# A two-layer macaron transformer on eight cores: rounding written out on VectorE, bf16 quantized weights in HBM, and other orders for LayerNorm and the output projections

## The chip, the cores and the metric

One Trainium2 chip (trn2), all 8 NeuronCores. Each core computes one sequence of the batch of eight, with the same program and no exchange between cores. The metric is the device time in microseconds (us) of the slowest core.

## What is computed

```python
x = x + 0.5 * ffn0(layernorm(x))     # call 1 of ffn_l0
x = x + attn0(layernorm(x))          # 16-head softmax attention, T = 2048, D = 1024
x = x + 0.5 * ffn0(layernorm(x))     # call 2 of ffn_l0, the same weights
x = x + 0.5 * moe1(layernorm(x))     # two of eight experts are ever used
x = x + attn1(layernorm(x))          # linear attention, D_KV = 512
x = x + 0.5 * moe1(layernorm(x))

def act_quant(x):                    # per token
    scale = 127.0 / clip(max(abs(x), axis=-1), 1e-05)
    return clip(round(x * scale), -128, 127) / scale
def weight_quant(w):                 # one scale for the whole matrix, result -1, 0 or 1 times it
    scale = 1.0 / clip(mean(abs(w)), 1e-05)
    return clip(round(w * scale), -1, 1) / scale
def ffn0(x):                         # w1: 4096 x 1024, w2: 1024 x 4096
    h = act_quant(x) @ weight_quant(w1).T
    h = silu(depthwise_conv1d(h, conv_w, conv_b))      # 3 taps along the sequence
    return act_quant(h) @ weight_quant(w2).T
```

## The kernel before

The activations x_sb stay in SBUF for the whole program as 8 chunks (dc) of 128 features by 2048 tokens in f32. Everything is feature-major: a matmul has a 128x128 weight tile as its stationary operand and 512 tokens as the moving one.

Order of the work. The program is written out by hand. `em.emit` (line 47) puts each instruction on the queue of its engine with the semaphore counts it waits for. On VectorE, ScalarE and GpSimd each instruction also waits for the one before it on its own engine (`self_sems`), so on an engine nothing overlaps with its predecessor. `guard()` is a wait for everything emitted so far, the DMAs too. The weight traffic (`w1sl`, `w2sl`, `wq1s`, `wq2s`, `slg`) is issued from GpSimd's queue (POOL), in order: a DMA that waits holds back those behind it. All small helpers have one line each: tt 214, tsc 219, stt 228, cp 236, red 241, act 252, mm 208, dma 197.

LayerNorm, `emit_ln` (line 460), six times. For each of 4 groups of 512 tokens and each of 8 chunks ScalarE makes a bf16 copy and a bf16 square in the one buffer `lnscr`, and two matmuls with a column of ones (`ln_ps`) sum them; the next pair of activations waits for these two matmuls. That is 32 steps per LayerNorm. Then come the statistics per token, two broadcasts through HBM (`bcast_tok`), and two VectorE operations of 2048 columns per chunk. The tags in `res_q` let a step start when its 512 tokens are final; for this the output projections and residual adds of attn_l0, moe_l1 and attn_l1 run with the token group `qb` outside and `dc` inside.

The feed-forward block, `ffn_l0` (line 550), twice.
- Quantizing the input: the maximum per token, its broadcast, then per chunk (128x2048) two VectorE operations, a multiply with int8 output (`xi8`) and a multiply back to bf16 (`xsc1`).
- For each of 4 token groups q: the H stage, 32 steps hc. A step is 8 matmuls into `H_ps[b]` (and 8 of one column for the right neighbour of the convolution), a small copy (`hlsv`), ScalarE's scaled copy `atmp`, four VectorE operations (`t1tmp`), and ScalarE's silu into `ysilu`. Then the maximum and broadcasts, and the O stage, again 32 steps hc: VectorE multiplies to int8 (`xi2`) and back to bf16 (`xsc2[b]`), PE does 8 matmuls into the 8 banks `O_ps`. Eight residual adds end the group.
- Weight tiles come from HBM as int8, are turned to bf16 by the DMA, and are loaded for two hc at a time (`slg`, 512 KB each, two buffers; `load1`, `load2`).

The ternary weights, `prep_weight` (line 308), are made during call 1 of ffn_l0 only. Pass 1 (`s_p1`, 64 pieces of 128x512 for each of w1 and w2) sums absolute values on ScalarE; `prep_pre` emits all 128 in the middle of the input quantization. `s_fin` makes the threshold from the sum, through several small DMAs. Pass 2 (`s_p2`, again 64 + 64 pieces) compares on VectorE and stores int8 to HBM from two buffers `g8`. `prep_drain(n)` emits the next n of the steps `s_fin`, `s_p2`, `s_end`: 10 ahead of the first H stage and 4 in each step of it, so all 132 are done in the H stage of group 0:

```python
tsc("vector", H["g8"][b], H["slab"][b], H["thp"][:, 0:1], None, ALU.is_ge)
tsc("vector", H["slab"][b], H["slab"][b], H["thp"][:, 1:2], None, ALU.is_le)
tt("vector", H["g8"][b], H["g8"][b], H["slab"][b], ALU.subtract)
gcons[b] = dma(cq[b], wdst, H["g8"][b])
```

The two attention blocks and the expert block are touched only in the order of their last projection.

## Time and profile before

| | us |
|---|---|
| median of the 2 runs shown (7142.35 to 7152.05) | 7147.2 |
| the profiled execution | 7073.03 |
| its span on its slowest core, core 1 | 7071.3 |
| spans of the eight cores | 7046.3 to 7071.3 |
| VectorE busy in that span | 2659.4 |
| PE busy in that span | 3289.9 |

The profiled execution is 74.2 us shorter than the median. The span runs from the first to the last instruction. Of the profile, "idle before" is time in which an engine did nothing just ahead of such an instruction, with what ended that time. The stages of call 1 of ffn_l0 can be told by the tiles: `xi8q` input quantization, `w1g` and `w2g` pass 2, `Hps` the H stage, `xi` with `Ops` the O stage.

### The profile page before, as it was taken

To read this page: it belongs to the slowest core of one execution; us is meant where nothing else is said; L and a number is where in the kernel's file an instruction comes from. 1 tells how busy PE (TensorE), PEld (TensorE's weight loads), DVE (VectorE), ACT (ScalarE), POOL (GpSimd) and SP (SyncE) were. 2 spreads that over 40 slices of the span, in tenths; PEclk is the share of its full clock that TensorE was granted. 3 is DMA by queue.
4 is the path that set the end of the run, shared out by engine and by line. 5 is a ranking of instruction groups with operands and counts; after the bars stand their busy time and mean duration, and the time that the engine had idled before them with its cause. 6 is when DMAs were issued, how large, how long until landed. Compare 5 with 4: busy or idle time off the path is not lost.

```text
span 7071.3 us, 55121 instructions; the slowest of 8 cores (7046.3 to 7071.3 us)
## 1 busy us (share of the span) xinstructions
PE 3289.9 (47%) x13238; PEld 1250.4 (18%) x13238; DVE 2659.4 (38%) x4180; ACT 1815.5 (26%) x2752; POOL 492.8 (7%) x828
## 2 busy tenths in 40 slices
PE   2022265465255555555555432556545264344345
PEld 0000022222021112211211111222211021122012
DVE  0655655555212222122212226555653331333223
ACT  2400111211225554665466221121122002000100
POOL 0332210000000000000000000001000000000000
PEclk9965587787577667666766756778776586676568
DMA  2632322122010000000000101212211010100022
GB/s 80 183 109 83 94 84 72 44 82 67 17 12 5 7 8 10 5 5 10 8 7 2 18 12 42 66 51 81 69 48 51 29 21 11 29 8 6 12 36 60
DMA packets 142962, 290.67 MB, mean 41 GB/s; under 512 B 35106, under 2 KB 42306, under 8 KB 138050
## 3 DMA queue, kind: packets, MB, share of 16 engines
q0 software_dynamic: 129088, 240.38, 13.3%
q1 hardware_dynamic: 13572, 46.77, 2.0%
q8 instruction: 127, 2.08, 0.1%
q14 instruction: 175, 1.43, 0.1%
HBM read 229.01 MB, written 17.25 MB: 35 GB/s over the span
## 4 chain that ended last, share of the span: by engine, by line
PE 25%; DVE 23%; ACT 22%; DMA 18%; issue 10%; ACTq 1%; DVEq 1%; POOLq 0%; SPq 0%; POOL 0%
ACT aE L252 14%; DVE t1tmp L228 6%; PE Ops L208 4%; ACT lnscr L252 3%; PE meps L208 3%; DVE aden L246 3%; DMA slg<-wq2s 3%; PE Hps L208 3%; PE ln_ps L208 3%; DMA w2sl<-w2h 2%; ACT atmp L252 2%; PE aqkps L208 2%; ACT ysilu L252 2%; PE mops L208 2%; DVE sv2bc L241 2%
## 5 line engine op out<-in xcount | busy, mean ns | idle before, releaser
L208 PE MATMUL Hps<-xsc,slg 128*128 128x512 bf16 (+1 forms) x3584 | 699.6, 348 | 1037.5 <-ACT ysilu L252 439.9
L252 ACT ACTIVATE aE<-aA 128x1024 bf16<-128x1024 f32 x512 | 523.9, 1023 | 394.3 <-PE aA L208 293.3
L252 ACT ACTIVATE aE<-asps 128x1024 bf16<-128x1024 f32 x512 | 523.8, 1023 | 392.9 <-PE asps L208 334.7
L252 ACT ACTIVATE lnscr<-x_sb 128x512 bf16<-128x512 f32 x384 | 241.5, 629 | 1420.5 <-PE ln_ps L208 597.1
L252 ACT ACTIVATE atmp<-Hps,cbsb,cw2sb 128x512 f32<-128x512 f32 x256 | 198.9, 777 | 1422.5 <-DVE hlsv L236 1388.7
L208 PE MATMUL Ops<-xsc,slg 128*128 128x512 bf16 x2048 | 484.7, 391 | 151.5 <-DVE xsc L214 105.7
L208 PEld LDWEIGHTS Hps<-xsc,slg 128*128 128x128 bf16 x3584 | 292.7, 110 | 1446.0 <-issue 1314.8
L208 PE MATMUL aA<-aKp,aQp 64*128 64x512 bf16 x1024 | 387.4, 575 | 285.6 <-ACT aE L252 256.4
L208 PE MATMUL asps<-aQ,aK 65*128 65x512 bf16 x1024 | 336.2, 415 | 254.1 <-DMA aQ<-aQp 230.9
L208 PE MATMUL ln_ps<-lnscr,onesbf 128*1 128x512 bf16 x384 | 193.6, 607 | 423.0 <-ACT lnscr L252 367.7
L228 DVE SCALAR_TENSOR_TENSOR t1tmp<-Hps,cw2sb,atmp 128x511 f32<-128x511 f32 (+1 forms) x512 | 247.7, 484 | 348.6 <-ACT atmp L252 321.3
L208 PE MATMUL apps<-aE,avtok 128*65 128x512 bf16 x1024 | 328.3, 403 | 86.8 <-ACT aE L252 45.2
L252 ACT ACTIVATE ysilu<-t1tmp 128x512 f32<-128x512 f32 x256 | 161.1, 629 | 625.0 <-DVE t1tmp L228 622.3
L214 DVE TENSOR_TENSOR ad<-ad,aacc 128x1 f32<-128x1 f32 x512 | 81.7, 160 | 618.1 <-ACT aE L252 618.1
L208 PE MATMUL meps<-mxln,mew 128*128 128x512 bf16 x1024 | 230.3, 388 | 153.2 <-DMA mew<-e0T 79.9
L236 DVE CAST aden<-apps 1x512 bf16<-1x512 f32 x64 | 44.1, 689 | 649.9 <-PE apps L208 626.9
L208 PEld LDWEIGHTS Ops<-xsc,slg 128*128 128x128 bf16 x2048 | 194.2, 100 | 440.6 <-issue 250.9
L214 DVE TENSOR_TENSOR xi<-ysilu,s2bc 128x512 int8<-128x512 f32 x256 | 177.2, 692 | 223.8 <-PE Ops L208 145.3
L208 PE MATMUL aqkps<-axln,aqk 128*128 128x512 bf16 x512 | 128.8, 419 | 172.1 <-DVE aout L214 157.7
L246 DVE RECIPROCAL aden<-aden 1x2048 bf16<-1x2048 bf16 x16 | 207.1, 12944 | 1.7
L228 DVE SCALAR_TENSOR_TENSOR t1tmp<-Hps,cw2sb,t1tmp 128x511 f32<-128x511 f32 x256 | 191.8, 749 | 27.6 <-DVE t1tmp L228 1.4
L208 PEld LDWEIGHTS aA<-aKp,aQp 64*128 64x128 bf16 x1024 | 101.0, 100 | 570.6 <-issue 555.8
(181 smaller groups left out, 3754.7 us busy)
## 6 DMA issues: line engine op xcount, KB each, us to landing
slg<-wq1s POOLq DMA_DIRECT2D x128, 512.0 KB, 3.7
slg<-wq2s POOLq DMA_DIRECT2D x128, 512.0 KB, 3.7
w1sl<-w1h POOLq DMA_DIRECT2D x128, 256.0 KB, 3.1
w2sl<-w2h POOLq DMA_DIRECT2D x128, 256.0 KB, 3.1
x_sb<-x SPq DMA_DIRECT2D x8, 1024.0 KB, 5.0
out<-x_sb SPq DMA_DIRECT2D x8, 1024.0 KB, 3.9
ln_rbc<-rowbuf SPq DMA_DIRECT2D x6, 1024.0 KB
ln_mrbc<-rowbuf SPq DMA_DIRECT2D x6, 1024.0 KB
```

The costliest lines, as they stand in the source:

```text
L208: tp=tile_position: e.matmul(o, l, r, start=a, stop=b, tile_position=tp),
L214: e.tensor_tensor(o, a, b, p), wait=wait, inc=inc)
L228: p=op0, q=op1: e.scalar_tensor_tensor(o, i, s, j, p, q),
L236: em.emit(eng, lambda e, o=out_ap, i=in_ap: e.tensor_copy(o, i), wait=wait, inc=inc)
L241: e.tensor_reduce(o, i, axis=AX.X, op=p, apply_absolute_value=a),
L246: em.emit(eng, lambda e, o=out_ap, i=in_ap: e.reciprocal(o, i), wait=wait, inc=inc)
L252: s=scale, a=accum: e.activation(o, i, f, bias=b, scale=s, accum_out=a),
```

## The change

Seven edits:
- Rounding. Each int8 multiply is replaced by a chain: multiply to f32, cast to int8 (`c8`, `c82`), subtract, compare the remainder with half-integers, and add the correction. The chain has 8 operations where KL is 1 (call 1, which has `pre`) and 12 where KL is 3 (call 2); before it was 2. It is in the input quantization (128x2048) and in every step of the O stage (128x512).
- Pass 1 is a VectorE reduce instead of a ScalarE activation.
- Pass 2 has five VectorE operations instead of three, into one f32 buffer `ptmp` shared by w1 and w2, which the next piece may write only when the store of the last one has landed (`ptmp_rd`). The store turns f32 to bf16.
- The quantized weights lie in HBM as bf16, and are loaded for one hc at a time (256 KB).
- The preparation steps are emitted as 3 per step of the H stage and 2 per step of the O stage.
- LayerNorm: per chunk, VectorE copies 2048 columns and ScalarE squares 2048 columns, then 8 matmuls; 8 steps instead of 32.
- The output projections run with `dc` outside and `qb` inside; `yconv` and `amax2p` have tiles of their own.

```diff
-    wq1s = nc.dram_tensor("wq1s", [HC, 128, DC * 128], I8)
+    wq1s = nc.dram_tensor("wq1s", [HC, 128, DC * 128], BF16)
...
-                act(H["slab"][k % 2][:, :], H["slab"][k % 2][:, :],
-                    AF.Abs, accum=H["part"][:, k:k + 1],
-                    wait=[ltags[k]], inc=Ssc)
+                red("vector", H["part"][:, k:k + 1], H["slab"][k % 2][:, :],
+                    ALU.add, absval=True, wait=[ltags[k]], inc=Sdv)
...
-                tsc("vector", H["g8"][b][:, :], H["slab"][b][:, :],
-                    H["thp"][:, 0:1], None, ALU.is_ge, wait=w0, inc=Sdv)
-                tsc("vector", H["slab"][b][:, :], H["slab"][b][:, :],
-                    H["thp"][:, 1:2], None, ALU.is_le, inc=Sdv)
-                tt("vector", H["g8"][b][:, :], H["g8"][b][:, :],
+                thv = bass.AP(H["thp"], 0, [[2, 128], [0, SW]])
+                if ptmp_rd[0] is not None:
+                    w0.append(ptmp_rd[0])
+                stt("vector", ptmp[:, 0:SW], H["slab"][b][:, :], 1.0,
+                    thv, ALU.mult, ALU.subtract, wait=w0, inc=Sdv)
+                stt("vector", H["slab"][b][:, :], H["slab"][b][:, :], 1.0,
+                    thv, ALU.mult, ALU.add, inc=Sdv)
+                tsc("vector", ptmp[:, 0:SW], ptmp[:, 0:SW], 0.0, None,
+                    ALU.is_ge, inc=Sdv)
+                tsc("vector", H["slab"][b][:, :], H["slab"][b][:, :], 0.0,
+                    None, ALU.is_le, inc=Sdv)
+                tt("vector", ptmp[:, 0:SW], ptmp[:, 0:SW],
                    H["slab"][b][:, :], ALU.subtract, inc=Sdv)
...
-                gcons[b] = dma(cq[b], wdst, H["g8"][b][:, :],
+                gcons[b] = dma(cq[b], wdst, ptmp[:, 0:SW],
                                wait=[(Sdv, Sdv.c)])
+                ptmp_rd[0] = gcons[b]
...
+                    for dc in range(DC):
+                        cp("vector", scr[:, 0:T], x_sb[:, dc * T:(dc + 1) * T],
+                           wait=(g0 if dc == 0 else [(Spe, Spe.c)]), inc=Sdv)
+                        act(scr[:, T:2 * T], x_sb[:, dc * T:(dc + 1) * T],
+                            AF.Square,
+                            wait=(g0 if dc == 0 else [(Spe, Spe.c)]),
+                            inc=Ssc)
...
+                    KL = 1 if pre is not None else 3
                     for dc in range(DC):
...
+                        tt("vector", xi8[:, :], e1, s_bc[:, :], ALU.mult,
                            wait=[b2] if dc == 0 else (), inc=Sdv)
...
-                            if hc % 2 == 1 and g + 2 < 16:
-                                load1(g + 2)
+                            if hc + 2 < HC:
+                                load1(hc + 2)
...
                         for hc in range(HC):
-                            g, b = hc // 2, hc % 2
+                            if drain:
+                                drain(2)
+                            g, b = hc, hc % 2
...
+                            e1 = ysilu[:, hc * QT:(hc + 1) * QT]
+                            tt("vector", xi2[:, :], e1, s2_bc[:, :],
                                ALU.mult,
                                wait=[b2, (Spe, o_pe[b])], inc=Sdv)
+                            cp("vector", c82[:, :], xi2[:, :], inc=Sdv)
+                            tt("vector", xi2[:, :], xi2[:, :], c82[:, :],
+                               ALU.subtract, inc=Sdv)
+                            tsc("vector", e1, xi2[:, :], 0.5, None,
+                                ALU.is_gt, inc=Sdv)
+                            for j in range(1, KL):
+                                stt("vector", e1, xi2[:, :], j + 0.5, e1,
+                                    ALU.is_gt, ALU.add, inc=Sdv)
+                            for j in range(KL):
+                                stt("vector", e1, xi2[:, :], -(j + 0.5),
+                                    e1, ALU.is_ge, ALU.add, inc=Sdv)
+                            tsc("vector", e1, e1, float(-KL), None,
+                                ALU.add, inc=Sdv)
+                            stt("vector", xi2[:, :], e1, 1.0, c82[:, :],
+                                ALU.mult, ALU.add, inc=Sdv)
                             tt("vector", xsc2[b][:, :], xi2[:, :],
                                sv2_bc[:, :], ALU.mult, inc=Sdv)
...
-                        for qb in range(4):
-                            for dc in range(DC):
-                                pw = dc % 2
+                        for dc in range(DC):
+                            for qb in range(4):
+                                pw = (dc * 4 + qb) % 2
```

VectorE at the start of the O stage of call 1, group 0, before (the small operations that end the scale computation, then the steps; `xi` is the int8 result, `xsc` the operand of the matmuls):

```order
L236 COPY trtmp<-bcps 4x128 x2
L214 TENSOR_TENSOR xi_43<-ysilu,s2bc 128x512
L214 TENSOR_TENSOR xsc_46<-xi_43,sv2bc 128x512
L214 TENSOR_TENSOR xi_43<-ysilu,s2bc 128x512
L214 TENSOR_TENSOR xsc_47<-xi_43,sv2bc 128x512
```

The same place in the changed kernel, from the last operation of a pass 2 piece of w2 on (`c` is the int8 cast):

```order
L214 TENSOR_TENSOR ptmp<-ptmp,w2sl 128x512
L214 TENSOR_TENSOR xi_42<-ysilu,s2bc 128x512
L236 CAST c_43<-xi_42 128x512
L214 TENSOR_TENSOR xi_42<-xi_42,c_43 128x512
L219 TENSOR_SCALAR ysilu<-xi_42 128x512
L228 SCALAR_TENSOR_TENSOR ysilu<-xi_42,ysilu 128x512
L219 TENSOR_SCALAR ysilu<-ysilu 128x512
L228 SCALAR_TENSOR_TENSOR xi_42<-ysilu,c_43 128x512
L214 TENSOR_TENSOR xsc_46<-xi_42,sv2bc 128x512
L228 SCALAR_TENSOR_TENSOR ptmp<-w2sl,w2th 128x512
```

Two operations between one matmul operand and the next have become eight, and in the first 13 steps two pieces of pass 2 stand between the steps.

VectorE in the H stage of group 0, before, around the four convolution operations of one step (`hlsv` to the last `t1tmp`) and the start of the first of four pieces of pass 2:

```order
L214 TENSOR_TENSOR w1g_19<-w1g_19,w1sl 128x512
L236 COPY hlsv<-Hps 128x1
L228 SCALAR_TENSOR_TENSOR t1tmp<-Hps,cw2sb,atmp 128x511
L228 SCALAR_TENSOR_TENSOR t1tmp<-Hps,cw2sb,atmp 128x1
L228 SCALAR_TENSOR_TENSOR t1tmp<-Hps,cw2sb,t1tmp 128x511
L228 SCALAR_TENSOR_TENSOR t1tmp<-hlsv,cw2sb,t1tmp 128x1
L219 TENSOR_SCALAR w1g_20<-w1sl,w1th 128x512
L219 TENSOR_SCALAR w1sl<-w1sl,w1th 128x512
L214 TENSOR_TENSOR w1g_20<-w1g_20,w1sl 128x512
```

The same place in the changed kernel:

```order
L236 COPY hlsv<-Hps 128x1
L228 SCALAR_TENSOR_TENSOR t1tmp<-Hps,cw2sb,atmp 128x511
L228 SCALAR_TENSOR_TENSOR t1tmp<-Hps,cw2sb,atmp 128x1
L228 SCALAR_TENSOR_TENSOR yconv<-Hps,cw2sb,t1tmp 128x511
L228 SCALAR_TENSOR_TENSOR yconv<-hlsv,cw2sb,t1tmp 128x1
L228 SCALAR_TENSOR_TENSOR ptmp<-w1sl,w1th 128x512
L228 SCALAR_TENSOR_TENSOR w1sl<-w1sl,w1th 128x512
L219 TENSOR_SCALAR ptmp<-ptmp 128x512
L219 TENSOR_SCALAR w1sl<-w1sl 128x512
L214 TENSOR_TENSOR ptmp<-ptmp,w1sl 128x512
L228 SCALAR_TENSOR_TENSOR ptmp<-w1sl,w1th 128x512
```

A piece has five operations, three pieces stand in a step where four stood, and each piece writes the same `ptmp`.

POOL's queue in the H stage of group 0 in the changed kernel (store of a piece, load of the piece two further on, and the weight tile for the H stage):

```order
L197 DMA slg<-wq1s 128x1024
L197 DMA wq1s<-ptmp 128x512
L197 DMA w1sl<-w1h 128x512
L197 DMA wq1s<-ptmp 128x512
L197 DMA w1sl<-w1h 128x512
L197 DMA wq1s<-ptmp 128x512
L197 DMA w1sl<-w1h 128x512
L197 DMA slg<-wq1s 128x1024
```

Before, `slg` was 128x2x1024 and stood after every eighth piece of pass 2; now it stands after every third.

## Rows read from the trace of the kernel before

**Rows 1.** The page's part 1: busy us of each engine, share of the span, instructions.
```profile
PE 3289.9 (47%) x13238; PEld 1250.4 (18%) x13238; DVE 2659.4 (38%) x4180; ACT 1815.5 (26%) x2752; POOL 492.8 (7%) x828
```

**Rows 2.** Windows: length, busy PE, PEld, DVE, ACT, POOL, clock, DMA share, GB/s.
```profile
975.00:1128.00 153.00, 85.87 (x512) 38.95 (x512) 81.50 (x162) 45.00 (x64) 9.82 (x14) 0.78 0.16 49
...
1158.00:1228.00 70.00, 60.24 (x256) 24.39 (x256) 44.30 (x64) 0.00 (x0) 9.83 (x14) 0.93 0.37 109
```

**Rows 3.** Timeline, first LayerNorm, steps 2 and 3: start, duration, instruction.
```profile
62.70 1.35 ACT L252 ACTIVATE lnscr<-x_sb 128x512 bf16<-128x512 f32 x2 [1.36 <-PE ln_ps L208]
...
65.30 1.35 ACT L252 ACTIVATE lnscr<-x_sb 128x512 bf16<-128x512 f32 x2 [1.25 <-PE ln_ps L208]
```

**Rows 4.** Groups by form, whole span: count, busy, mean ns, idle before.
```profile
L252 ACT ACTIVATE aE<-aA 128x1024 bf16<-128x1024 f32 x512 | 523.9, 1023 | 394.3 <-PE aA L208 293.3 <-ACT aE L252 88.6 <-DVE ad L214 4.3
...
L252 ACT ACTIVATE lnscr<-x_sb 128x512 bf16<-128x512 f32 x384 | 241.5, 629 | 1420.5 <-PE ln_ps L208 597.1 <-PE lops L208 464.3 <-DVE x_sb L214 259.6
...
L214 DVE TENSOR_TENSOR xi<-ysilu,s2bc 128x512 int8<-128x512 f32 x256 | 177.2, 692 | 223.8 <-PE Ops L208 145.3 <-DMA sv2bc<-rowbuf 76.5 <-DVE xsc L214 2.0
...
L228 DVE SCALAR_TENSOR_TENSOR x_sb<-Ops,q2col,x_sb 128x512 f32<-128x512 f32 x64 | 48.0, 750 | 36.8 <-PE Ops L208 22.6 <-DVE x_sb L228 14.2
...
L214 DVE TENSOR_TENSOR xi8q<-xlnf,s1bc 128x2048 int8<-128x2048 f32 x16 | 36.7, 2292 | 34.0 <-DMA sv1bc<-rowbuf 32.5
...
L219 DVE TENSOR_SCALAR w1sl<-w1sl,w1th 128x512 f32<-128x512 f32 x64 | 31.2, 488 | 6.9
...
L236 DVE CAST lsbf<-ls 128x512 bf16<-128x512 f32 x60 | 25.6, 427 | 6.2
```

**Rows 5.** VectorE's timeline, call 1: input quantization, threshold, first piece, end of group 0's H stage.
```profile
285.44 2.29 DVE L214 TENSOR_TENSOR xi8q<-xlnf,s1bc 128x2048 int8<-128x2048 f32 x1 [20.06 <-DMA sv1bc<-rowbuf]
287.84 2.29 DVE L214 TENSOR_TENSOR xsc<-xi8q,sv1bc 128x2048 bf16<-128x2048 int8 x1
...
329.16 0.22 DVE L241 TENSOR_REDUCE w1pp<-w1pp 128x1 f32<-128x64 f32 x1 [0.17 <-DVE hlsv L265]
...
362.12 0.49 DVE L219 TENSOR_SCALAR w1g<-w1sl,w1th 128x512 int8<-128x512 f32 x1 [15.65 <-DMA w1sl<-w1h]
...
868.63 13.86 DVE L241 TENSOR_REDUCE s2bc<-ysilu 128x512 f32<-128x8192 f32 x1 [0.90 <-ACT ysilu L252]
```

**Rows 6.** Pieces of w1 in pass 1: duration ns min/median/max, first and last start.
```profile
L252 ACT ACTIVATE w1sl<-w1sl x64: 629/630/631, 154.2 to 326.6; 128x512 f32<-128x512 f32 x64
```

**Rows 7.** Timeline in the H stage of group 0, one step of hc.
```profile
442.41 0.69 DVE L214 TENSOR_TENSOR w1g<-w1g,w1sl 128x512 int8<-128x512 int8 x1
443.28 0.16 DVE L236 COPY hlsv<-Hps 128x1 f32<-128x1 f32 x1 [0.17 <-DVE w1g L214]
...
443.65 0.54 POOL L197 DMA_DIRECT2D wq1s<-w1g  x1 [1.01 <-DVE hlsv L236]
...
447.04 0.49 DVE L219 TENSOR_SCALAR w1g<-w1sl,w1th 128x512 int8<-128x512 f32 x1 [0.38 <-DVE t1tmp L228]
```

**Rows 8.** DMA to landing of w1g's stores, then DMA issues: KB each, us to landing.
```profile
DMA to landing us min/median/max: 1.8/1.8/7.9
...
slg<-wq2s POOLq DMA_DIRECT2D x128, 512.0 KB, 3.7
...
awv<-wqkvT POOLq DMA_DIRECT2D x16, 128.0 KB, 2.9
```

**Rows 9.** VectorE's timeline, O stage of group 1: its first step and its first residual add.
```profile
1160.86 0.69 DVE L214 TENSOR_TENSOR xi<-ysilu,s2bc 128x512 int8<-128x512 f32 x1 [9.88 <-DMA sv2bc<-rowbuf]
...
1228.30 0.75 DVE L228 SCALAR_TENSOR_TENSOR x_sb<-Ops,q2col,x_sb 128x512 f32<-128x512 f32 x1 [2.48 <-PE Ops L208]
```

**Rows 10.** Timeline, H stage of call 2: two steps that follow on each other.
```profile
4396.03 0.16 DVE L236 COPY hlsv<-Hps 128x1 f32<-128x1 f32 x1 [0.17 <-DVE t1tmp L228]
...
4396.87 3.75 PE L208 MATMUL Hps<-xsc,slg 128*128 128x512 bf16 x16 [1.09 <-ACT ysilu L252]
...
4400.73 0.16 DVE L236 COPY hlsv<-Hps 128x1 f32<-128x1 f32 x1 [0.81 <-PE Hps L208]
```

131 lines of the change are left out of this document (58 added, 73 removed).

## Prediction

> **What bounds the kernel now.** I read the page's first part, then the windows by stage, then the timeline inside one step of each stage the diff touches, because no engine fills the span (PE is busy 47% of it, VectorE 38% [rows 1]). The bound changes from stage to stage, so each edit is priced in its own stage.
> - O stage: of 70 us PE is busy 60.24 and VectorE 44.30 [rows 2]. From its first VectorE operation to the first residual add it takes 1228.30 - 1160.86 = 67.4 us [rows 9], 2.1 us for each of 32 steps. PE bounds it, VectorE has about a third to spare.
> - H stage of groups 1 to 3: neither is full (PE 85.87, VectorE 81.50 of 153) [rows 2]; a ring of PE, ScalarE and VectorE sets the step.
> - H stage of group 0: VectorE. In one step pieces of pass 2 and the convolution follow each other on it without a gap worth naming [rows 7]; the stage lasts 868.63 - 362.12 = 506.5 us [rows 5].
> - LayerNorm sums: a ring of ScalarE (1.35 us for a pair) and PE (ScalarE waits 1.25 for two matmuls), period 65.30 - 62.70 = 2.60 us [rows 3], 32 times = 83.2 us, with VectorE idle.
>
> **Prices of VectorE operations at 512 columns.** Two-tensor multiply or subtract 0.692 [rows 4]. Cast within SBUF 0.427 [rows 4]. Compare or add with a constant: the row with a pointer scalar takes 0.488, the cast without one 0.427; the new ones have a plain constant, I take 0.43. Scalar-tensor-tensor: the trace has it only with a pointer scalar, 0.750, against 0.692 for the two-tensor form [rows 4]; the new ones have a constant, I take 0.692, the other end is 0.750. From one operation to the next passes 287.84 - 285.44 - 2.292 = 0.107 [rows 4, 5]. So 0.80 for an operation with two tensors and 0.54 for one with one. At 2048 columns the first is 2.292 [rows 4], 2.40 with the gap. For the second I bound from both sides. A column costs the first form (2.292 - 0.692)/1536 = 1.04 ns; the cast is shorter by 0.265 at 512 columns, half of 512 x 1.04, so it streams at 0.52 ns a column: 0.427 + 1536 x 0.52 = 1.23. The other end is 2.292. I take 1.23, 1.33 with the gap, as the row at 512 says.
>
> **O stages.** Call 1: 5 operations with two tensors and 3 with one in a step, 5 x 0.80 + 3 x 0.54 = 5.6, with the wait at its head 5.67 us, over twice PE's 2.1. So VectorE bounds: 32 x 5.67 + 3 for the last matmuls = 184.5, against 67.4: +117 per group, +468 for four. Call 2 (KL 3) has 4 more: 5.67 + 3.20 = 8.87, 32 times + 3 = 287: +220 per group, +880. The first part of this work is hidden in VectorE's idle ahead of `xi`, 145.3 us for PE in all 256 steps [rows 4]; that is already in the difference, since 67.4 contains it.
>
> **Slabs of one hc.** A load waits for the matmuls of hc and is needed for hc + 2. At the slowest, the matmuls of a step last 3.75 [rows 10] and a load of twice the size lands in 3.7 [rows 8]: 7.5 us, less than two steps in H (8.7 on the mean, below) and far less than two O steps (11.3). No cost; if cover were gone, each 0.1 us would be 25 us in all. bf16 in HBM doubles what is read, but the DMA share is 0.16 in H and 0.37 in O [rows 2] and O gets slower: nothing. `yconv` and `amax2p` take no wait away that ends last: `t1tmp` already waits for the `atmp` behind the silu. Nothing.
>
> **Input quantization.** Call 1 per chunk 5 x 2.40 + 3 x 1.33 = 16.0, eight times 128 against 16 x 2.40 = 38. Call 2: 9 x 2.40 + 3 x 1.33 = 25.6, 205 against 38: +166. PE waits for it in both.
>
> **Pass 1.** On ScalarE 128 pieces lay from 154.2 to 327 [rows 6], that is 1.35 us each for 0.63 of work: the loads set the pace. They lay beside VectorE's LayerNorm and quantization, so they cost almost nothing. Now they stand in VectorE's queue ahead of the quantization. A reduce of 512 is at least 0.5 and, like the other 1-element-per-cycle operations, about 0.7, so the loads still set the pace: 172 us. With the loads gone the broadcast wait (20.06 [rows 5]) shrinks by about 10. Quantization starts at 285.4 - 41 (LayerNorm, below) + 172 - 10 = 406.4, ends at 534.4. The threshold takes 362.12 - 329.16 = 33 [rows 5], so pass 2 starts at 567.4 instead of 362.1: +205.
>
> **Pass 2.** A piece is 3 x 0.80 + 2 x 0.54 = 3.47 us (before, three operations, 2.0). The added wait is that for the last store. From VectorE's end (442.41 + 0.69 = 443.10) to the DMA's issue at 443.65 pass 0.55 [rows 7]. Landing: 1.8 for the 64 KB int8 store, 2.9 for a load with the same cast and tile (awv), 3.7 for the largest slab [rows 8]. I take 2.7, near the row with the same bytes, a little less since it is a store. With 0.1 to come back the stall is 3.35. Queued behind it on VectorE are the rest of the pieces and the convolution, for which ScalarE and PE wait. The first piece of a step is spared: its store lands beside the convolution work, 447.04 - 443.28 = 3.76 [rows 7]. The next load on POOL lands about 4.2 us after a piece and is needed 10 us after it: hidden.
> The Trainium skill, DMA: Bandwidth & Descriptors, Anatomy of one DMA, puts a DMA from GpSimd at 2.0 us + bytes/436 GB/s; 256 KB of f32 would give an estimate of 2.6, and this sum 8 us less. No run here shows this store.
> Sum of group 0's H stage: 9 pieces up front 9 x 6.82 = 61; 94 pieces in the steps x 3.47 = 326; 63 stalls x 3.35 = 211; 32 x 3.76 = 120; the threshold of w2 33; first maximum 14. That is 765, against 506.5: +259. In the O stage 25 pieces are left: 25 x 3.47 + 12 x 3.35 = +127.
>
> **LayerNorm.** ScalarE at 2048 columns: (1.023 - 0.629)/512 from the two rows [rows 4] gives 1.81, four times 0.629 gives 2.5; the first row reads PSUM, I take 1.9. VectorE's copy (1.23) lies beside it. Then 7 of 8 matmuls at 0.43, which is 512 columns at 1.2 GHz, and the hand-overs, 1.25 - 2 x 0.43 = 0.39 [rows 3]: 1.9 + 3.0 + 0.39 = 5.3 us, 8 times 42.4, against 83.2. Saved 40.8 each; one is counted above, five are -204. With qb outside the old kernel could start sums early, but the matmuls of LayerNorm stand behind the whole projection in PE's queue and the single `lnscr` lets only one pair run ahead: the lost overlap is at most 2 us each, and dc outside costs nothing (the same matmuls, the same adds). If PE got the faster level there, the step would be 3.8 and each LayerNorm 12 less.
>
> **Sum.** Call 1: 205 + 259 + 127 + 468 = 1059. Call 2: 166 + 880 = 1046. LayerNorms -204. Together +1901 on the profiled execution's 7073 (its span and 2 us around it): 8974. That execution is 74 below the median of the runs shown, so 9048, rounded 9050.
>
> **Rivals.**
> 1. *Hidden after all (the other side).* VectorE is idle 62% of the span, 4400 us [rows 1], and the added busy time is near 1760. If the rounding chains and pieces filled idle time and did not stand between a matmul and its operand, only LayerNorm would show: 7147 - 6 x 40.8 = 6902. It would decide where the added work of a step is under the idle time before `xi`, 145.3/256 = 0.57 us [rows 4]; the added work is 4 to 7 us. 1%.
> 2. *Slow H steps.* PE's granted clock is 0.78 in H and 0.93 in O [rows 2]. The mean step is 4.34 us (the 153 us of the stage [rows 2] less 14 for the first maximum, over 32), and there are steps of 4400.73 - 4396.03 = 4.70 [rows 10], where 16 matmuls take 3.75 and the copy waits for PE, which is then at 1.2 GHz. After the change PE waits more in the O stages; if this put all of H at the lower level, 7 stages x 32 x (4.70 - 4.34) = +81: 9131. Against it: within H nothing changes. 15%.
> 3. *Dear scalar-tensor-tensor.* At 0.750 there are 1024 of them in the O stages and 256 in pass 2, x 0.058 = +74: 9124. 15%.
> 4. *VectorE starves GpSimd's DMAs.* If stores and loads were held up beside a busy VectorE, each exposed store could take the worst landing of its kind, 7.9 instead of 2.7 [rows 8]: 84 x 5.2 = +437: 9487. Against it: the median store landed in 1.8, its minimum, while VectorE ran compares; and the new store flies while VectorE stands still. 4%.
> The Trainium skill, SBUF — State Buffer, Who interferes with whom, has this as a lock: a copy, cast or tensor-scalar in its two-port form shuts GpSimd out while it runs. By that rule the median landing should have been longer than the minimum; the trace does not agree.
>
> **How the numbers follow.** The forecast has 65%. The range takes the store's landing (1.8 to 3.7: -76 to +84), the LayerNorm step (-70), rivals 2 and 3, and the 74 us between execution and median: 8880 to 9240. A change of 2%, 143 us, is about what can be told here. All cases but the first are slower by far more: faster 1%, same 1%, slower 98%.
>
> **What would show it.** Right: VectorE busy near 4420 us; O steps of 5.7 and 8.9 us with PE's matmuls released by `xsc`; pass 1 on VectorE at about 1.35 a piece, released by DMA; in group 0's H stage VectorE waiting for `wq1s` about 3.3 us between pieces; LayerNorm sums of 42 us in place of 83. Wrong: O steps released by `slg`; a constant's compare at 0.69 instead of 0.43, which at 3 per O step would add 768 x 0.26 = 200 us; or H stages that differ from 153.

## The result and the profile after

The changed kernel takes 8889.6 us (median of 11 runs, 8863.9 to 8901.1) where the kernel before takes 7109.7 us (10 runs): a ratio of 1.2511, with a 95% interval of 1.2468 to 1.2553. The forecast was 9050, with a range of 8880 to 9240. Its direction and its cause hold; the time is 160 us lower than forecast, 10 us above the lower end of the range. (One experiment below, the LayerNorm alone, has no interval: in three of its four runs cores of one die had a lower clock and took longer.)

The page's part 1 of the kernel after, the row that answers to [rows 1]:

```profile
PE 3611.9 (41%) x13238; PEld 1327.5 (15%) x13238; DVE 4423.4 (50%) x6788; ACT 1574.2 (18%) x2160; POOL 587.3 (7%) x1084
```

VectorE's busy time rose by 1764 us, and the span by 1802 (8873.5 - 7071.3). That these two are nearly equal is partly chance: some of VectorE's new work is covered, and its waits for the stores are new. So I go by stages again. The windows after (length, then busy us and instructions of PE, PEld, DVE, ACT, POOL, then clock, DMA share, GB/s) of an H stage, an O stage of call 1, an O stage of call 2, the first LayerNorm sums and pass 1:

```profile
1622.00:1776.00 154.00, 83.79 (x512) 38.41 (x512) 81.42 (x163) 45.02 (x64) 16.09 (x30) 0.80 0.17 52
1807.00:1994.00 187.00, 99.32 (x256) 30.39 (x256) 151.55 (x256) 0.00 (x0) 16.53 (x30) 0.66 0.15 42
5596.00:5885.00 289.00, 112.73 (x256) 33.39 (x256) 240.38 (x384) 0.00 (x0) 16.09 (x30) 0.59 0.09 28
60.00:93.00 33.00, 19.54 (x64) 5.27 (x64) 8.59 (x7) 15.05 (x8) 0.42 (x1) 1.00 0.05 16
201.00:362.00 161.00, 0.74 (x2) 0.18 (x2) 88.12 (x131) 0.00 (x0) 67.56 (x126) 0.50 0.69 206
```

Against [rows 2] the H stage is unchanged (154 us, clock 0.80, where it was 153 and 0.78). In the O stages VectorE has gone from 44.30 of 70 us to 151.55 of 187 and 240.38 of 289, and with the 0.107 us behind each of its 256 and 384 instructions that is 179 and 281: it is full but for a short wait at the head of each step. In pass 1 VectorE is busy for 88 of 161 us and waits for the loads in between, so the loads set the pace.

VectorE's timeline after, where the first LayerNorm's broadcast lands, then for the stages of [rows 5] (quantization, threshold, first piece, end of group 0's H stage) and then the first residual add of four O stages (group 0 and 3 of call 1, group 0 and 3 of call 2):

```profile
117.69 2.29 DVE L214 TENSOR_TENSOR xlnf<-x_sb,ln_rbc 128x2048 f32<-128x2048 f32 x1 [10.66 <-DMA ln_mrbc<-rowbuf]
...
372.23 2.29 DVE L214 TENSOR_TENSOR xi8q<-xlnf,s1bc 128x2048 f32<-128x2048 f32 x1 [10.63 <-DMA sv1bc<-rowbuf]
...
500.98 0.22 DVE L241 TENSOR_REDUCE w1pp<-w1pp 128x1 f32<-128x64 f32 x1 [0.18 <-DVE hlsv L265]
...
533.00 0.69 DVE L228 SCALAR_TENSOR_TENSOR ptmp<-w1sl,w1th 128x512 f32<-128x512 f32 x1 [16.05 <-DMA w1sl<-w1h]
...
1263.64 13.86 DVE L241 TENSOR_REDUCE s2bc<-ysilu 128x512 f32<-128x8192 f32 x1 [0.90 <-ACT ysilu L252]
...
1614.13 0.75 DVE L228 SCALAR_TENSOR_TENSOR x_sb<-Ops,q2col,x_sb 128x512 f32<-128x512 f32 x1 [2.75 <-PE Ops L208]
...
2754.66 0.75 DVE L228 SCALAR_TENSOR_TENSOR x_sb<-Ops,q2col,x_sb 128x512 f32<-128x512 f32 x1 [4.01 <-PE Ops L208]
...
5885.17 0.75 DVE L228 SCALAR_TENSOR_TENSOR x_sb<-Ops,q2col,x_sb 128x512 f32<-128x512 f32 x1 [4.01 <-PE Ops L208]
...
7332.29 0.75 DVE L228 SCALAR_TENSOR_TENSOR x_sb<-Ops,q2col,x_sb 128x512 f32<-128x512 f32 x1 [4.01 <-PE Ops L208]
```

And the same broadcast and the same four residual adds in the kernel before:

```profile
175.52 2.29 DVE L214 TENSOR_TENSOR xlnf<-x_sb,ln_rbc 128x2048 f32<-128x2048 f32 x1 [18.49 <-DMA ln_mrbc<-rowbuf]
...
967.47 0.75 DVE L228 SCALAR_TENSOR_TENSOR x_sb<-Ops,q2col,x_sb 128x512 f32<-128x512 f32 x1 [2.91 <-PE Ops L208]
...
1751.06 0.75 DVE L228 SCALAR_TENSOR_TENSOR x_sb<-Ops,q2col,x_sb 128x512 f32<-128x512 f32 x1 [2.66 <-PE Ops L208]
...
4605.19 0.75 DVE L228 SCALAR_TENSOR_TENSOR x_sb<-Ops,q2col,x_sb 128x512 f32<-128x512 f32 x1 [2.69 <-PE Ops L208]
...
5392.85 0.75 DVE L228 SCALAR_TENSOR_TENSOR x_sb<-Ops,q2col,x_sb 128x512 f32<-128x512 f32 x1 [2.78 <-PE Ops L208]
```

These marks cut both executions into the same seven stretches. The difference in each, beside what the prediction's terms give for it (in us):

| stretch | forecast | measured |
|---|---|---|
| start to pass 2 (533.00 - 362.12) | +205 | +170.9 |
| H stage of group 0 (730.6 for 506.5) | +259 | +224.1 |
| to group 0's residual add (350.5 for 98.8) | 127 + 117 = +244 | +251.7 |
| groups 1 to 3 of call 1 (1140.5 for 783.6) | 3 x 117 = +351 | +356.9 |
| to call 2's first residual add (3130.5 for 2854.1) | 166 + 220 - 2 x 41 = +304 | +276.4 |
| groups 1 to 3 of call 2 (1447.1 for 787.7) | 3 x 220 = +660 | +659.5 |
| to the end (1541.2 for 1678.4) | -3 x 41 = -122 | -137.2 |
| sum | +1901 | +1802 |

Inside one O step of call 1 VectorE's timeline has the eight operations (the first five are shown, and the first of the next step), 1818.03 - 1812.32 = 5.71 us from step to step (5.67 forecast):

```profile
1812.32 0.69 DVE L214 TENSOR_TENSOR xi<-ysilu,s2bc 128x512 f32<-128x512 f32 x1 [0.17 <-DVE xsc L214]
1813.11 0.43 DVE L236 CAST c<-xi 128x512 int8<-128x512 f32 x1
1813.64 0.69 DVE L214 TENSOR_TENSOR xi<-xi,c 128x512 f32<-128x512 f32 x1
1814.44 0.43 DVE L219 TENSOR_SCALAR ysilu<-xi 128x512 f32<-128x512 f32 x1
1814.97 0.69 DVE L228 SCALAR_TENSOR_TENSOR ysilu<-xi,ysilu 128x512 f32<-128x512 f32 x1
...
1818.03 0.69 DVE L214 TENSOR_TENSOR xi<-ysilu,s2bc 128x512 f32<-128x512 f32 x1 [0.24 <-DVE xsc L214]
```

The groups of the kernel after (count, busy, mean ns, idle before and what ended it) give the prices and the new waits:

```profile
L208 PE MATMUL Ops<-xsc,slg 128*128 128x512 bf16 x2048 | 851.6, 591 | 1264.4 <-DVE xsc L214 1264.4
...
L228 DVE SCALAR_TENSOR_TENSOR ysilu<-xi,ysilu 128x512 f32<-128x512 f32 x768 | 531.6, 692 | 81.0 <-DVE ysilu L219 1.4
...
L228 DVE SCALAR_TENSOR_TENSOR ptmp<-w1sl,w1th 128x512 f32<-128x512 f32 x64 | 44.3, 692 | 157.2 <-DMA wq1s<-ptmp 135.4 <-DMA w1sl<-w1h 16.1 <-DVE yconv L228 5.4
...
L228 DVE SCALAR_TENSOR_TENSOR ptmp<-w2sl,w2th 128x512 f32<-128x512 f32 x64 | 44.3, 692 | 155.2 <-DMA wq2s<-ptmp 132.4 <-DMA w2sl<-w2h 14.2 <-DVE yconv L228 4.5
...
L241 DVE TENSOR_REDUCE w1pp<-w1sl 128x1 f32<-128x512 f32 x64 | 43.9, 686 | 25.3 <-DMA w1sl<-w1h 21.7 <-DVE w2pp L241 3.4 <-DVE tok_b L219 0.2
```

All of PE's idle time ahead of the second matmul, 1264 us, is ended by `xsc`. The waits for stores are 135.4 us at w1's pieces and 132.4 at w2's.

### The profile page after: what moved, and what is told of

Its sections match the earlier page's. It is cut to its first block, busy times and chain, and to the rows that moved or that the text cites. A ratio compares the mean times of both kernels' runs of the same rounds, so it can differ in the third digit from the quotient of the medians.

```text
span 8873.5 us, 60484 instructions; the slowest of 8 cores (8833.2 to 8873.5 us)
## 1 busy us (share of the span) xinstructions
PE 3611.9 (41%) x13238; PEld 1327.5 (15%) x13238; DVE 4423.4 (50%) x6788; ACT 1574.2 (18%) x2160; POOL 587.3 (7%) x1084
## 4 chain that ended last, share of the span: by engine, by line
DVE 42%; PE 17%; ACT 16%; DMA 13%; issue 10%; DVEq 1%; ACTq 1%; POOLq 0%; POOL 0%; SPq 0%
ACT aE L252 11%; DVE ysilu L228 6%; DVE xi L214 4%; PE meps L208 3%; DVE ysilu L219 3%; DVE xsc L214 2%; DVE t1tmp L228 2%; DVE yconv L228 2%; DVE aden L246 2%; PE Hps L208 2%; DVE xi L228 2%; ACT atmp L252 2%; PE aqkps L208 1%; DVEq L71 1%; PE mops L208 1%
## 5 line engine op out<-in xcount | busy, mean ns | idle before, releaser
L208 PE MATMUL Ops<-xsc,slg 128*128 128x512 bf16 x2048 | 851.6, 591 | 1264.4 <-DVE xsc L214 1264.4
L228 DVE SCALAR_TENSOR_TENSOR ysilu<-xi,ysilu 128x512 f32<-128x512 f32 x768 | 531.6, 692 | 81.0 <-DVE ysilu L219 1.4
L208 PEld LDWEIGHTS Ops<-xsc,slg 128*128 128x128 bf16 x2048 | 254.3, 133 | 1857.2 <-issue 1833.1
L252 ACT ACTIVATE ln_scr<-x_sb 128x2048 bf16<-128x2048 f32 x48 | 91.7, 1910 | 1594.3 <-DVE x_sb L214 488.7
L208 PE MATMUL meps<-mxln,mew 128*128 128x512 bf16 x1024 | 251.0, 414 | 142.7 <-DMA mew<-e0T 73.6
L197 POOL DMA_DIRECT2D slg<-wq2s x256 | 138.1, 540 | 2024.8 <-PE Ops L208 1728.0
L252 ACT ACTIVATE ysilu<-yconv 128x512 f32<-128x512 f32 x256 | 161.1, 629 | 624.7 <-DVE yconv L228 619.2
L214 DVE TENSOR_TENSOR xi<-ysilu,s2bc 128x512 f32<-128x512 f32 x256 | 177.2, 692 | 120.4 <-DVE xsc L214 59.3
L197 POOL DMA_DIRECT2D slg<-wq1s x256 | 137.3, 536 | 1430.0 <-PE Hps L208 1108.0
L228 DVE SCALAR_TENSOR_TENSOR yconv<-Hps,cw2sb,t1tmp 128x511 f32<-128x511 f32 x256 | 191.8, 749 | 27.8 <-DVE t1tmp L228 1.7
```

Of the source, the lines that this page charges most:

```text
L197: em.emit(ch.eng, lambda e, d=dst, s=src: e.dma_start(d, s), wait=w, inc=sm, inc_n=16)
L208: tp=tile_position: e.matmul(o, l, r, start=a, stop=b, tile_position=tp),
L214: e.tensor_tensor(o, a, b, p), wait=wait, inc=inc)
L228: p=op0, q=op1: e.scalar_tensor_tensor(o, i, s, j, p, q),
L252: s=scale, a=accum: e.activation(o, i, f, bias=b, scale=s, accum_out=a),
```

## The experiments

Each kernel ran in three rounds beside the kernel before. "Against after" is the difference of medians to 8889.6. The length of a LayerNorm's sums is always taken from the first write of the scratch tile to the end of the last matmul; in the kernel before it is 82 to 83 us, 496 for all six.

### The LayerNorm alone, in the kernel before

The loop of the changed kernel, put into the kernel before. Its scratch tile lies where `r_bc` and `mr_bc` lie later, since 8 KB more don't fit beside them.

```diff
+                    scr = scx.enter_context(nc.sbuf_tensor(
+                        uid("ln_scr"), [128, 2 * T], BF16))
+                    for dc in range(DC):
+                        cp("vector", scr[:, 0:T], x_sb[:, dc * T:(dc + 1) * T],
...
+                    scx.close()
+                    r_bc = lsb("ln_rbc", [128, T], F32)
```

> The kernel before with one part of the change alone: the LayerNorm sums in 8 steps of 2048 columns (copy on VectorE beside square on ScalarE). Theory (the change's LayerNorm takes 33 to 37 us where the old one takes 83 to 86, and this stands alone on the path in all six LayerNorms): -250 to -300 us, so 6810 to 6860. Rival A (the prediction's own term, -40.8 each): -204 to -245. Rival B (the sums became shorter only because the kernel around them changed, for instance because TensorE was granted a higher clock after slower stages): under -150, with a step of 5.3 us.

Measured: 6770.3 us in the one run that can be compared, 312 below the lowest run of before in the same job (7082.6). That is one run against one, and 12 more than the theory's upper end. In the profile the six sums together take 203 to 213 us on cores 0 to 3 (most of them 33 to 35 each) and 226 on core 6, shown below: 270 to 293 less than 496. The term is that of the theory, -45 to -49 a LayerNorm, and not the -41 of the prediction. Rival B falls, as these are the lengths of the changed kernel too (205 to 215 for six, over its eight cores). The timeline of TensorE in the first LayerNorm shows why the forecast of 42.4 was too high:

```profile
63.95 3.81 PE L208 MATMUL ln_ps<-ln_scr,onesbf 128*1 128x512 bf16 x8 [1.48 <-DVE ln_scr L236]
69.24 3.42 PE L208 MATMUL ln_ps<-ln_scr,onesbf 128*1 128x512 bf16 x8 [1.48 <-DVE ln_scr L236]
74.14 0.38 PE L208 MATMUL ln_ps<-ln_scr,onesbf 128*1 128x512 bf16 x1 [1.48 <-DVE ln_scr L236]
74.81 1.67 PE L208 MATMUL ln_ps<-ln_scr,onesbf 128*1 128x512 bf16 x7 [0.30 <-ACT ln_scr L252]
77.96 0.38 PE L208 MATMUL ln_ps<-ln_scr,onesbf 128*1 128x512 bf16 x1 [1.48 <-DVE ln_scr L236]
78.63 1.67 PE L208 MATMUL ln_ps<-ln_scr,onesbf 128*1 128x512 bf16 x7 [0.30 <-ACT ln_scr L252]
```

The first steps have the forecast's 5.29 us (69.24 - 63.95), with matmuls that follow each other at 0.43 us. After three of them the matmuls follow at 0.21 us, TensorE's upper level, and a step is 77.96 - 74.14 = 3.82 us. It isn't so in every LayerNorm: on cores 4 and 5 of this execution the last five take 41 to 42 us each, with steps of 4.2 to 5.7 us to their end.

### The same with both passes on ScalarE

```diff
-                        cp("vector", scr[:, 0:T], x_sb[:, dc * T:(dc + 1) * T],
-                           wait=(g0 if dc == 0 else [(Spe, Spe.c)]), inc=Sdv)
+                        act(scr[:, 0:T], x_sb[:, dc * T:(dc + 1) * T],
+                            AF.Identity,
+                            wait=(g0 if dc == 0 else [(Spe, Spe.c)]), inc=Ssc)
```

> As the one with the new LayerNorm alone, but the copy is on ScalarE too, ahead of the square: tells what the second engine gives and what the longer steps give. Theory (copy 1.91, square 1.91, then four matmuls of square, about 5.0 to 5.3 us a step): 41 us a LayerNorm, -43 each, -255 us. Rival (the gain is that two engines work at once; longer steps alone give nothing): within 1% of before.

Measured: ratio 0.9887 (0.9804 to 0.9969), medians 7039.9 for 7121.2, sums of 62 to 65 us. The theory's number was missed; the rival's "within 1%" was missed narrowly and lies within the interval. The timeline shows why: the first matmul waits for the count that ScalarE's semaphore has after both activations, so for the second of them too.

```profile
1775.76 3.96 ACT L252 ACTIVATE ln_scr<-x_sb 128x2048 bf16<-128x2048 f32 x2 [5.47 <-PE ln_ps L208]
...
1779.87 3.57 PE L208 MATMUL ln_ps<-ln_scr,onesbf 128*1 128x512 bf16 x8 [4.21 <-ACT ln_scr L252]
```

ScalarE's 3.96 and TensorE's 3.57 stand one behind the other, 7.8 us a step. The next kernel has the sum's four matmuls ahead of the square's, and they wait for the copy alone:

```diff
+                        cpt = (Ssc, Ssc.c)
...
-                               wait=([(Ssc, Ssc.c)] +
+                               wait=([cpt] +
```

> As the LayerNorm with copy and square both on ScalarE in steps of 2048, but the four matmuls of the sum wait for the copy alone (in the run before they waited for the square too, and each step was 3.96 us of ScalarE and then 3.56 us of TensorE). Theory (step length and overlap both count; step = 1.91 + 1.91 + four matmuls of 0.21 to 0.43 and some 0.3): 4.9 to 5.8 us a step, sums of 39 to 47 us, -35 to -43 each against before's 82: -210 to -255 us, 6850 to 6900. Rival (only work on a second engine pays): 58 us as before, -80 us.

Measured: ratio 0.9669 (0.9618 to 0.9721), 6915.9 us, 209 below before in its job; sums of 48 to 50 us, 6.1 us a step (ScalarE's next pair starts at 1771.66 and 1777.73). That is the lower edge of the theory. The matmuls stayed at 0.43 us in most steps (granted clock 0.57 in the second LayerNorm's window). Of the 47 to 49 us that a LayerNorm gained on cores 0 to 3 of the kernel above, then, 33 come without VectorE: 19 from steps four times as long, and the rest of the 33 from the overlap of the sum's matmuls with the square. The other 14 to 16 come with VectorE's copy, through the shorter step and the higher clock together.

### The same with the scratch tile double

```diff
+                        o = (dc % 2) * 2 * T
+                        w0 = (g0 if dc < 2 else [(Spe, pe_t[dc - 2])])
```

The four sum matmuls come first, then the four of the square, as above.

> As the one with the new LayerNorm alone, but with two copies of the scratch tile, so that VectorE and ScalarE fill one while TensorE reads the other. Theory (steps at ScalarE's 1.91 us, 8 of them and an end, about 18 us for the sums): -65 us for each of six LayerNorms, -390 us against before, about 6720. Rival (TensorE becomes the bound with 8 matmuls of 0.43 us a step, as at the lower clock): 3.4 us a step, 29 us, -330 us.

Measured: ratio 0.9488 (0.9415 to 0.9562), medians 6764.3 for 7121.2 us. The sums take 19 to 23 us, near the theory's 18, and 496 - 123 = 373 less lies within the interval (the medians differ by 357; the rival's -330 lies within it too, but steps of about 3 us are only the first one or two of a LayerNorm, the others are 1.7 to 2.1). ScalarE runs without a gap, and TensorE is at its upper level:

```profile
1729.56 8.08 ACT L252 ACTIVATE ln_scr<-x_sb 128x2048 bf16<-128x2048 f32 x4 [1.64 <-PE ln_ps L208]
...
1729.73 5.83 PE L208 MATMUL ln_ps<-ln_scr,onesbf 128*1 128x512 bf16 x26
```

Four squares in 8.08 us are 2.02 each, so ScalarE is the bound; 26 matmuls in 5.83 us are 0.22 each.

### The rounding alone, in the O stages of the kernel before

```diff
-                xi2 = fsb("xi2", [128, QT], I8)
+                xi2 = fsb("xi2", [128, QT], F32)
+                c82 = fsb("c82", [128, QT], I8)
...
+                            cp("vector", c82[:, :], xi2[:, :], inc=Sdv)
+                            tt("vector", xi2[:, :], xi2[:, :], c82[:, :],
+                               ALU.subtract, inc=Sdv)
...
```

> The kernel before with the written-out rounding in the O stages alone (8 operations a step in call 1, 12 in call 2, in place of 2); the input quantization, pass 1, pass 2 and the LayerNorms stay as they were, so that only the activations of the second matmul are rounded in the new way. Theory (the prediction's terms): 4 x 117 + 4 x 220 = +1348 us, about 8420 on its profiled execution, O stages of 187 and 289 us. Rival A (part of the rounding hides beside the stages' matmuls or beside the weight pieces): under +1150. Rival B (the prediction's O terms are too small and another one too large): over +1450.

Measured: ratio 1.1915 (1.1827 to 1.2004), medians 8472.7 for 7121.2: +1351 for the +1348 of the two terms. The O stage's window is that of the kernel after (187 us), and nothing of the LayerNorm, the slabs or the pieces is in it:

```profile
1658.00:1845.00 187.00, 98.93 (x256) 30.22 (x256) 152.09 (x257) 0.00 (x0) 10.68 (x15) 0.66 0.13 40
```

### The rounding taken out of the changed kernel

The reverse: both quantizations have their two int8 operations again, all else of the change stays.

```diff
-                            cp("vector", c82[:, :], xi2[:, :], inc=Sdv)
-                            tt("vector", xi2[:, :], xi2[:, :], c82[:, :],
-                               ALU.subtract, inc=Sdv)
...
```

> The changed kernel with the two int8 multiplications back in both quantizations, all else of the change kept; rounding is as in the kernel before. Theory (the prediction's terms taken away: 91 + 166 for the two input quantizations, 468 + 880 for the O stages): -1605 us against the changed kernel, about 7285. Rival A (the weight pieces in the O stage of group 0 and the rounding there cover each other, so that less comes back): -1500. Rival B (what is left, VectorE's pass 1 and 2, costs more than the prediction has it): over 7400.

Measured: ratio 1.0505 (1.0427 to 1.0583), median 7452.3: -1437 against after, 168 less than the theory, and less than rival A's too. Rival B's number (over 7400) is met, but not for its reason. Most of the missing time is in the O stages: from the first to the last `xsc`, the seven after group 0's take 85 to 89 us where they take 64 to 68 in before, 7 x 21 = 147. Of the other 21, 10 are a pass 1 of 168 us for the changed kernel's 158; the rest is open. The groups of this kernel name what ended PE's waits there:

```profile
L208 PE MATMUL Ops<-xsc,slg 128*128 128x512 bf16 x2048 | 519.5, 404 | 419.4 <-DVE xsc L214 245.5 <-DMA slg<-wq2s 172.2
```

So the slabs of one hc, which cost nothing beside the rounding, cost once it is gone. In the changed kernel no wait of these matmuls is put down to `slg`; here it is 172.2 us.

### The small slabs, drains and loop order alone, in the kernel before

```diff
-                slg = [fsb("slg", [128, 2 * DC * 128], BF16)
+                slg = [fsb("slg", [128, DC * 128], BF16)
                        for _ in range(2)]
...
-                            if hc % 2 == 1 and g + 2 < 16:
-                                load2(g + 2)
+                            if hc + 2 < HC:
+                                load2(hc + 2)
...
-                                drain(4)
+                                drain(3)
```

> The kernel before with the edits that the prediction priced at nothing or by pieces moved: slabs for one hc instead of two (still int8), 3 pieces drained in an H step and 2 in an O step, dc as the outer loop of the output projections. Theory: small slabs and loop order cost nothing; the 25 or so pieces that move into the O stage of group 0 cost there about what they cost in the H stage or less: 0 to -60 us against before. Rival (small slabs land late, or a projection waits for more): +50 us or more, with waits of TensorE on slg in the H and O stages.

Measured: ratio 1.0197 (1.0141 to 1.0253), +140 us, where I had written 0 to -60: the rival is right, but for the H stages, whose seven later ones take 142 to 146 us from the first to the last silu, as in before. TensorE's timeline in the O stage of group 1:

```profile
1200.64 3.61 PE L208 MATMUL Ops<-xsc,slg 128*128 128x512 bf16 x16 [1.96 <-DMA slg<-wq2s]
...
1205.75 3.61 PE L208 MATMUL Ops<-xsc,slg 128*128 128x512 bf16 x16 [1.49 <-DMA slg<-wq2s]
```

Two hc take 5.11 us where before took 4.2. A load is issued when its slab has been read and has one hc's 2.0 us to land; it lands in 2.6. Seven O stages of 81 to 86 us for 64 to 68 are 7 x 18 = +126. Four slabs of one hc (the memory of the old two) test this:

```diff
                slg = [fsb("slg", [128, DC * 128], BF16)
-                       for _ in range(2)]
+                       for _ in range(4)]
...
-                            if hc + 2 < HC:
-                                load2(hc + 2)
+                            if hc + 4 < HC:
+                                load2(hc + 4)
```

> As the kernel with one-hc slabs, but four of them in place of two (the same memory as the two two-hc slabs of before), so that a load is issued four hc ahead. Theory (in an O stage with two one-hc slabs each load is issued as its slab is read out and has one hc's 2.0 us to land, but takes 2.6 us; with four it has three hc): the seven undisturbed O stages go from 81 to 86 us back to 64 or 65, -120 to -135 us against the one with two, so 7090 to 7115, level with before. Rival (the smaller transfers themselves are dear, or GpSimd issues too slowly at 0.53 us and more each): the O stages stay over 78 us.

Measured: ratio 0.9974 (0.9942 to 1.0007), medians 7109.1 for 7124.7; the O stages take 61 to 65 us. The groups of PE, first with two slabs, then with four:

```profile
L208 PE MATMUL Ops<-xsc,slg 128*128 128x512 bf16 x2048 | 515.2, 401 | 324.5 <-DMA slg<-wq2s 164.3 <-DVE xsc L214 159.5
```

```profile
L209 PE MATMUL Ops<-xsc,slg 128*128 128x512 bf16 x2048 | 521.4, 414 | 158.7 <-DVE xsc L215 150.1 <-issue 1.6 <-DMA slg<-wq2s 0.4
```

164.3 us of waits for slabs became 0.4, with the same transfers of the same size (median landing 2.6 us in both). The distance of the load ahead is the cost, not the size of the transfer. Pieces drained 3 and 2 and dc outside cost nothing that shows in the total.

### Two temporary tiles for the weight pieces

```diff
-                if ptmp_rd[0] is not None:
-                    w0.append(ptmp_rd[0])
+                ptm = H["ptmp"][k % 2]
+                if ptmp_rd[k % 2] is not None:
+                    w0.append(ptmp_rd[k % 2])
```

> The changed kernel with two temporary tiles for the weight pieces, used in turn, in place of one: VectorE waits for the store before the last. Theory (83 waits of 3.0 to 3.3 us for the last store, 268 us in all, go, and the work under them is VectorE's own): -230 to -270 us, about 8640; H steps of group 0 from 22.8 to about 14 us. Rival (the pieces come no faster than GpSimd's queue loads and stores them, about 4 us each as in the kernel before, and the wait is put down to another transfer): -60 to -130 us, with waits on w1sl or w2sl in their place.

Measured: ratio 1.2199 (1.2134 to 1.2264), 8656.1 us, -233 against after. Group 0's H stage ends its pieces 142 us sooner (first to last activation 509 us for 651), its O stage is 45 us shorter, and the rest comes in the first pieces. Of the 267.8 us of waits for stores none shows any more, but waits for loads have grown: at w1 to 29.8 + 6.2 from 16.1, at w2 to 27.3 from 14.2. 268 - 33 = 235 is what was measured. The rows of w1:

```profile
L229 DVE SCALAR_TENSOR_TENSOR ptmp<-w1sl,w1th 128x512 f32<-128x512 f32 x32 | 22.2, 692 | 35.5 <-DMA w1sl<-w1h 29.8 <-DVE yconv L229 2.9 <-DVE w2pt L215 2.8
...
L229 DVE SCALAR_TENSOR_TENSOR w2pt<-w1sl,w1th 128x512 f32<-128x512 f32 x32 | 22.2, 692 | 14.0 <-DMA w1sl<-w1h 6.2 <-DVE ptmp L215 5.0 <-DVE yconv L229 2.5
```

### Pass 1 back on ScalarE in the changed kernel

```diff
-                red("vector", H["part"][:, k:k + 1], H["slab"][k % 2][:, :],
-                    ALU.add, absval=True, wait=[ltags[k]], inc=Sdv)
-                cons[k % 2] = (Sdv, Sdv.c)
+                act(H["slab"][k % 2][:, :], H["slab"][k % 2][:, :],
+                    AF.Abs, accum=H["part"][:, k:k + 1],
+                    wait=[ltags[k]], inc=Ssc)
+                cons[k % 2] = (Ssc, Ssc.c)
```

> The changed kernel with pass 1 (the absolute sums of the weight pieces) back on ScalarE, so that it runs beside VectorE's input quantization. Theory (pass 1 takes 158 us in which VectorE would have quantized): the quantization starts at about 215 us, not at 372, and pass 2 at about 390, not at 533: -130 to -150 us. Rival (pass 1 is bound by the loads and the quantization's start by something else): within 50 us of the changed kernel.

Measured: ratio 1.2299 (1.2233 to 1.2365), 8731.7 us, -158 against after, 8 more than the theory's upper end. The quantization begins at 225.90 in place of 372.23, and pass 2 at 385.94 in place of 533.00, which is 147 us sooner:

```profile
225.90 2.29 DVE L214 TENSOR_TENSOR xi8q<-xlnf,s1bc 128x2048 f32<-128x2048 f32 x1 [17.88 <-DMA sv1bc<-rowbuf]
...
385.94 0.69 DVE L228 SCALAR_TENSOR_TENSOR ptmp<-w1sl,w1th 128x512 f32<-128x512 f32 x1 [16.13 <-DMA w1sl<-w1h]
```

It begins 11 us later than the theory's 215, since the broadcasts take longer with pass 1's loads beside them: VectorE waits 16.92 us for that of the LayerNorm and 17.88 for this one, and 10.66 and 10.63 in the changed kernel.

### Together

Two temporary tiles, pass 1 on ScalarE and the double scratch tile, in the changed kernel; its edits are those above.

> The changed kernel with two temporary tiles, pass 1 on ScalarE, and the LayerNorm scratch double: the rounding, the slabs and the rest of the change stay. Theory (the three act in different stretches and add up: -233 and -158 as measured alone, and 6 x 14 for LayerNorm sums of 19 us in place of 33): about 8415 us. Rival (the two that touch the weight pieces overlap: pass 2 that starts earlier runs against loads that a second temporary would have used too): over 8480.

Measured: ratio 1.1854 (1.1813 to 1.1895), 8456.4 us, -433 against after. The parts alone sum to -475; 42 us are not accounted for, and the result lies between the theory's 8415 and the rival's 8480. By the profile each stage has its part: H of group 0 is 508 us from first to last silu, the sums are 19 to 22.

And for the kernel before: the double scratch tile, four small slabs, the drains and the loop order.

> The kernel before with the double-buffered LayerNorm of 2048 columns, four one-hc slabs, 3 and 2 pieces drained in H and O steps, and dc as the outer loop of the projections. Theory (slabs and drains are level with before, the LayerNorm gives its -63 each): -350 to -400 us against before, the same as the one with the LayerNorm alone within 40 us. Rival (one-hc slabs keep a cost): 50 us or more above it.

Measured: ratio 0.9385 (0.9341 to 0.9429), 6697.1 us, -428 where -350 to -400 were expected. It is the fastest of all and beats both kernels: the sums take 19 to 22 us, and the seven O stages 61 to 62. It is 67 us below the one with the LayerNorm alone, more than the 40 expected; since the two ran on different chips, only part of that may be the slabs and drains (O stages 3 us shorter, seven times).

## Why the prediction was right, and where it was off

**O stages: right.** +468 and +880 were forecast. The rounding alone gives +1351 for +1348, with stages of 187.4 and 288.9 us (184.5 and 287). The prices at constants, taken as 0.692 and 0.43, are 0.692 and 0.427 to 0.429 in the trace, so rival 3 (dear scalar-tensor-tensor) is refuted. The two prices were choices between neighbouring rows, argued and not measured before; both came out.

**Slabs of one hc: right in this kernel, for the reason given.** The prediction said that a load has two long steps and that cover is all that hides it. Without the rounding the cover is gone, and the price is 18 to 21 us per O stage. It had given only "each 0.1 us would be 25 us" and no size; the size is about 0.6 us a step.

**Input quantization: right.** From 372.23 to the threshold's reduction at 500.98 pass 128.8 us, for 128.

**Pass 1: right in kind, two terms mis-sized.** "The loads still set the pace: 172 us" took the pace of 1.35 us a piece that pass 1 had on ScalarE. On VectorE its 128 pieces from 200.6 to 358.5 are 1.23 each, 158 us. The loads landed no faster to speak of (median 3.34 us for 3.42), so why the pace differs is not shown; without the rounding it was 1.31. "They cost almost nothing" was wrong too. With pass 1's loads gone from beside them, the first LayerNorm's broadcast is waited for 10.66 us in place of 18.49, and another small transfer 1.55 in place of 4.80; only the wait that the prediction named fell as it said (20.06 to 10.63). In all eleven kernels here with pass 1 on ScalarE the LayerNorm's wait is 16.9 to 20.7 us, in the three with pass 1 on VectorE 10.7 to 13.2. These 14 and 11 us, and the first LayerNorm, whose sums ended 50 us earlier for the 41 of the forecast, are the 34 us of the first stretch. Putting pass 1 back yields 147, which confirms where it lay.

**Pass 2: right in kind, its term mis-sized.** The landing was taken as 2.7 and the stall, as time added to a piece, as 3.35. The chain of waits of the kernel after, from the end of one piece to the next, has:

```profile
542.01 0.70 DVE ptmp L214
542.75 0.48 issue
543.25 2.36 DMA wq1s<-ptmp
545.70 0.70 DVE ptmp L228
```

So 2.36, and 3.0 us from piece to piece where 0.107 would pass anyway: 2.9 added. In group 0's H stage 71 such waits of 3.01 on the mean are 71 x 2.9 = 206 us, where the prediction had 72 x 3.35 = 241. That is the whole of the 35 us by which the stage was overestimated. In its O stage the 12 waits are longer, 4.5 us on the mean: the store stands behind a slab's load in GpSimd's queue and is in most cases issued 1.2 us after the piece instead of 0.5, and it lands in 3.1. These 12 cost 53 us for the 40 of the sum, and the stretch came out 8 over it. Two temporary tiles remove the waits and 233 us. The Trainium skill, DMA: Bandwidth & Descriptors, Anatomy of one DMA, gave an estimate of 2.6 for this store from the 256 KB of f32 that are read; from the 128 KB that the profile lists for it the same formula gives 2.3. The trace has a median of 2.36 for the 128 stores.

**LayerNorm: mechanism right, the term mis-sized.** "Then 7 of 8 matmuls at 0.43" holds in five of the six LayerNorms of the profiled core for the first one or two steps only; after them it is 0.21 and the step 3.82, the 3.8 that the prediction named as the case of the faster level and did not take. The sixth is otherwise. Its steps go between 4.2 and 5.3 us to the end, with a granted clock of 0.61, and its sums take 41.5 us, near the 42.4 of the prediction (a window, its columns as above):

```profile
8342.00:8380.00 38.00, 26.11 (x64) 6.25 (x64) 8.59 (x7) 13.37 (x7) 0.00 (x0) 0.61 0.00 0
```

On core 4 it is the same (40.7 us), on the other six cores the sixth takes 34 to 36 like the rest; why is not shown. The six sums of 34 to 42 us together are 214 where before has 496: 282 saved for the 245 of the forecast, 37 us of the miss. In the kernel before the pairs of matmuls, 2.6 us apart, stayed at the lower level's times ([rows 3], and the same period at 1800 us).

**The last step.** The prediction added 74 us for the distance of the profiled execution of before to the median of the two runs shown. For after this distance is 15 (8889.6 - 8875.1), and the median of ten runs of before lies only 37 above its profiled execution (7109.7 - 7073.0). About 60 of the 160 us are this; 99 are the terms above, 25 of pass 1, 35 of the stalls and 37 of the LayerNorms, with small remainders of both signs. These three and the distance all went the same way, to a shorter time, and the range held by 10 us only, with a lower end that had been set by these same terms.

**The rivals.** 1 (hidden) falls with 1264 us of PE's waits on `xsc`. 2 (slow H steps) falls: the H stage is 154 us at clock 0.80, for 153 at 0.78. 3 is refuted by its price. 4 (VectorE starves GpSimd's DMAs) falls: the stores land in 2.3 to 5.4 us, median 2.4, and the rival had 7.9. The stores fly while VectorE stands still, but the slabs of the O stages don't: they are issued and land beside a VectorE that is full, in a median of 2.85 us (4.5 at the most), and in 2.94 with the rounding taken out. So the lock that the Trainium skill has in SBUF — State Buffer, Who interferes with whom, shows in no landing time here.
